# Two post-norm transformer layers on one core: the last gate/up step in halves, the high products of the first projection first, its weights in one piece, and new orders of the steps

## The reference, cut to what matters

```python
x = L0_attn_x                                   # (4, 256, 256)
x = _layernorm(x + _L0_attn_ref(x, w_project, w_out))              # 16 heads of 16, causal softmax
x = _layernorm(x + _L0_ffn_ref(x, gate_w, up_w, down_w, ...))      # silu(g) * u, 704 wide, ternary weights and scales
x = _layernorm(x + _L1_attn_ref(x, Wq, bq, Wk, bk, Wv, bv, Wo, bo))
x = _layernorm(x + _L1_ffn_ref(x, W_up, W_gate, W_down))           # 1024 wide, weights quantised to -1, 0, 1 times a scale
```

## Time and profile before

| | us |
|---|---|
| median of 3 runs | 256.35 (256.03 to 258.0) |
| profiled execution, its own time | 255.42 |
| its span, first to last instruction | 253.5 |
| PE busy | 240.6 |
| VectorE busy | 204.3 |
| GpSimd busy | 167.1 |
| ScalarE busy | 161.4 |

### The profile page before, as it was taken

One profiled execution on the slowest core, in us unless ns is written; L12 is line 12 of the kernel. 1 busy time (PEld: TensorE's weight loads), 2 busy tenths in 40 slices (PEclk: granted clock), 3 DMA queues, 4 the chain that ended last, 5 costly groups with the idle time before them and its releaser, 6 DMA issues.

```text
span 253.5 us, 6724 instructions
## 1 busy us (share of the span) xinstructions
PE 240.6 (95%) x2398; PEld 216.3 (85%) x2398; DVE 204.3 (81%) x599; ACT 161.4 (64%) x290; POOL 167.1 (66%) x218
## 2 busy tenths in 40 slices
PE   8998989999999999999999898998999999999991
PEld 8997967877789989989999897765788888999990
DVE  2477976999776876889999998998999975767664
ACT  4682465469889979627444567848788484555551
POOL 8763080528769854998637186599878885675663
PEclk9999999999999999999999999999999999999998
DMA  6867768542234343245626046055010000000003
GB/s 164 277 193 203 216 175 241 152 120 79 76 98 109 109 129 119 85 145 144 187 85 189 3 122 189 31 153 145 0 45 3 4 3 0 3 35 8 3 0 124
DMA packets 23312, 26.39 MB, mean 104 GB/s; under 512 B 3184, under 2 KB 18288, under 8 KB 23280
## 3 DMA queue, kind: packets, MB, share of 16 engines
q1 hardware_dynamic: 23136, 25.71, 35.2%
q10 hardware_dynamic: 144, 0.26, 0.3%
HBM read 12.20 MB, written 1.05 MB: 52 GB/s over the span
## 4 chain that ended last, share of the span: by engine, by line
PE 71%; POOL 6%; DVE 5%; DMA 5%; ACT 5%; issue 4%; SPq 2%; POOLq 0%; ACTq 0%
PE psum L566 9%; PE psum L567 8%; PE psum L568 8%; PE psum L686 6%; PE psum L661 5%; PE psum L741 5%; PE psum L742 5%; DMA k_stack<-k_part 3%; PE psum L629 3%; PE psum L689 2%; PE psum L633 2%; PE psum L664 2%; POOL hidden L1253 2%; PE psum L775 2%; PE psum L638 2%
## 5 line engine op out<-in xcount | busy, mean ns | idle before, releaser
L857 ACT ACTIVATE probs<-psum 128x768 f32<-128x768 f32 x64 | 49.1, 809 | 11.9 <-PE psum L667 5.9
L1253 POOL TENSOR_TENSOR hidden<-hf,hidden 128x512 fp32r<-128x512 f32 x24 | 31.6, 1320 | 13.5 <-ACT hidden L899 13.5
L1221 POOL TENSOR_SCALAR_AFFINE_SELECT probs<-probs 128x512 f32<-128x512 f32 x48 | 32.3, 688 | 10.1 <-ACT probs L857 9.7
L1009 DVE TENSOR_REDUCE block_max<-psum 128x6 f32<-128x768 f32 x32 | 28.9, 946 | 6.0 <-PE psum L633 5.9
L661 PE MATMUL psum<-q_stack,k_stack 98*128 98x256 bf16 x128 | 28.6, 274 | 2.1 <-DMA q_stack<-maxT_lo 1.0
L1020 DVE CUSTOM_DVE_ANT_0 masked<-psum,mask 128x256 bf16<-128x256 f32 x64 | 26.7, 418 | 1.6 <-issue 0.9
L1106 DVE SCALAR_TENSOR_TENSOR hf<-th,psum 128x512 f32<-128x512 f32 x28 | 18.9, 677 | 9.8 <-ACT th L888 3.9
L566 PE MATMUL psum<-xT_hi,gu_hi 128*128 128x256 f32 x88 | 25.3, 288 | 0.0
L567 PE MATMUL psum<-xT_lo,gu_hi 128*128 128x256 f32 x88 | 24.9, 283 | 0.0
L568 PE MATMUL psum<-xT_hi,gu_lo 128*128 128x256 f32 x88 | 24.9, 283 | 0.0
L664 PE MATMUL psum<-q_stack,k_stack 98*128 98x128 bf16 x128 | 24.7, 218 | 0.0
(11 more groups left out here) (167 smaller groups left out, 919.9 us busy)
## 6 DMA issues: line engine op xcount, KB each, us to landing
q_stack<-q_part SPq DMA_DIRECT2D x48, 128.0 KB, 2.7
k_stack<-k_part SPq DMA_DIRECT2D x48, 128.0 KB, 2.4
raw<-f SPq DMA_DIRECT2D x24, 256.0 KB, 3.0
raw<-a SPq DMA_DIRECT2D x8, 256.0 KB, 3.2
raw<-f0gu SPq DMA_DIRECT2D x4, 352.0 KB, 4.1
x<-x_nat SPq DMA_DIRECT2D x4, 256.0 KB, 5.4
raw<-f0dn SPq DMA_DIRECT2D x3, 256.0 KB, 3.0
out<-x SPq DMA_DIRECT2D x3, 256.0 KB, 2.3
```

The costliest lines, as they stand in the source:

```text
L857: nc.scalar.activation(probs[(n - 1) % 4][:, :, :], place(key)[:, :, 0:T + P], ACT.Exp, scale=SC).then_inc(exp_done, 1)
L1009: nc.vector.tensor_reduce(block_max[b % 2][:, 2 * i:2 * i + 2, 1:4], both(key)[:, :, 0:3 * P].rearrange("p j (c t) -> p j c t", t=P), mybi ...
L1221: pool.affine_select(out=diag, in_=diag, compare_op=ALU.is_ge, fill=0.0, base=0, pattern=[[0, 2], [0, 2], [1, P]], channel_multiplier=-1). ...
L1253: pool.tensor_tensor(hidden[(n - 1) % NHID][1][:, :, :], hf[n % 2][:, :].rearrange("p (a t) -> p a t", a=2), hidden[(n - 1) % NHID][0][:, ...
```

## The change

It has five parts.

1. QK:000 and QK:001 do their products in another order: four high by high products, which wait for the high parts alone, then four with xT_lo, then four with wa_lo. The number stays 12.
2. The four quarters of the weights a0, and those of a1, lie in memory so that a quarter is one row of 2 KB per partition; before, it was two rows of 1 KB.
3. The last gate/up step, GU:133, becomes GE:130 and GE:131, one tile of the hidden width each (8 matmuls, tanh of 256 columns, two products of 256 columns), HI:133 becomes HE:130 and HE:131, D:133 becomes DE:130 and DE:131 (4 matmuls each).
4. The last layer norm: VectorE does both halves' residuals, then both statistics, both aggregates and both additions of EPS, GpSimd the two powers; ScalarE normalises and stores the first half (NT:130), VectorE and SP the second.
5. All five lists of steps and BANKS are new.

```diff
 VECTOR_STEPS = """
-    XPARTS:000 PREPA:000-1 XPARTS:010 QK:000-1 XPARTS:020 XPARTS:030 QK:010 PREPA:002 QK:011 QK:020-1 PREPA:003
-    S:000-7 MB:000 S:010 MX:000 QK:030-1 S:011-6 SCALES:000 UT:000 IV:000 S:017 MB:010 S:020-1 MX:010 S:022 YM:000
+    PREPA:000-1 XPARTS:000 XPARTS:010 QK:000-1 XPARTS:020 QK:010-1 PREPA:002 QK:020-1 XPARTS:030 PREPA:003 S:000-7
+    MB:000 QK:030 S:010 MX:000 QK:031 S:011-5 SCALES:000 UT:000 IV:000 S:016-7 S:020 MB:010 S:021 UT:001 MX:010
...
 TENSOR_STEPS = """
-    QK:000 XI:010 QK:001 QK:010 XI:020 XI:030 QK:011 QK:020-1 V:000 V:010 S:000-4 QK:030 S:005-7 QK:031 S:010 MX:000
-    V:020 S:011-3 ST:000-1 S:014-5 ST:002-3 S:016 PV:000-1 ST:004-7 S:017 S:020-2 MX:010 PV:002-3 S:023-4 V:030
+    QK:000 XI:010 QK:001 XI:020 QK:010 XI:030 QK:011 QK:020-1 V:000 V:010 S:000-5 QK:030 S:006-7 QK:031 S:010 MX:000
+    S:011 V:020 S:012-4 ST:000 S:015 ST:001-3 S:016 PV:000-1 ST:004-7 S:017 S:020-1 PV:002-3 MX:010 S:022-5 V:030
...
-    GU:010-1 XT:020 XT:100 O:030 GU:012 QK:100 GU:020 D:010 XT:030 D:011-2 GU:021 QK:101 GU:022 XT:110 GU:030
-    QK:110-1 S:100-1 GU:031 S:102-3 D:020-1 S:104-5 D:022 GU:032 S:106-7 D:030-1 S:110 XT:120 V:100 S:111-2 MX:100
+    GU:012 GU:020 QK:100 XT:030 D:010-2 GU:021 QK:101 GU:022 XT:110 GU:030 QK:110-1 S:100-1 GU:031 S:102-3 D:020-2
+    S:104-5 GU:032 D:030 S:106-7 XT:120 D:031 S:110 V:100 MX:100 S:111 QK:120 S:112 D:032 S:113 QK:121 S:114 V:110
...
-    D:113 XT:230 GU:123 GU:130-1 D:120-2 GU:132-3 D:123 D:130-3
+    GU:130 D:120 GU:131 D:121-2 GU:132 D:123 GE:130-1 D:130-2 DE:130-1
...
 SCALAR_STEPS = """
...
-    GU:121 HI:120-1 XT:230 GU:122-3 GU:130 HI:122 GU:131 HI:123 HI:130-1 GU:132-3 HI:132-3 LN:310 LN:320
+    HI:121 XT:230 GU:122-3 GU:130 HI:122-3 GU:131 HI:130-1 GU:132 GE:130 HI:132 GE:131 HE:130-1 LN:310 LN:320 NT:130
...
 GPSIMD_STEPS = """
...
-    LN:020 LN:100 YT:030 HI:010 TERN:100 LN:030 TERN:101 HI:011 TERN:102 HI:012 SPLIT:100 TERN:103 LN:110 TERN:104-5
-    HI:020 SPLIT:101 HI:021-2 TERN:106 SPLIT:110 HI:030 SPLIT:111 HI:031 LN:120 HI:032 PREP1:003 TERN:107 LN:130
-    SPLIT:120-1 XC:100 ST:100-4 TERN:108 ST:105-7 XC:110 SPLIT:130-1 ST:110-5 YT:100 ST:116 TERN:109 ST:117 ST:120-1
+    HI:001-2 ST:035-7 LN:020 LN:100 YT:030 HI:010 TERN:100 LN:030 TERN:101 HI:011-2 TERN:102-3 SPLIT:100 LN:110
+    TERN:104 HI:020 TERN:105 SPLIT:101 HI:021 TERN:106 SPLIT:110 HI:022 HI:030 SPLIT:111 TERN:107 LN:120 HI:031-2
+    PREP1:003 LN:130 SPLIT:120-1 ST:100 XC:100 ST:101-2 XC:110 ST:103-7 SPLIT:130 TERN:108 ST:110 SPLIT:131 ST:111-5
...
 SYNC_STEPS = """
-    LOAD:001 LOAD:003 QK:000 LOAD:002 QK:001 MID:000-1 LO:000-1 QK:010 MID:010 LO:010 MID:011 QK:011 LO:011 LO:020
-    RAW:000-1 LOAD:000 MX:000 ML:000 LO:021 QK:020 MID:020-1 QK:021 RAW:002-3 MID:030 QK:030 MX:010 ML:010 MID:031
+    LOAD:001 QK:000-1 LOAD:003 LO:000-1 MID:000-1 MID:010 LO:010 QK:010-1 LO:011 MID:011 RAW:000-1 LO:020 LOAD:002
+    LOAD:000 MX:000 ML:000 LO:021 QK:020-1 MID:020-1 RAW:002-3 QK:030 MID:030-1 MX:010 ML:010 LO:030 QK:031 LO:031
...
-            c = slice(n * D, (n + 1) * D)
-            queue.dma_start(raw_a[:, :, c], a0[:, :, c]).then_inc(a0_in[n], 16)
+            queue.dma_start(raw_a[n], a0[:, n * KT * D:(n + 1) * KT * D]).then_inc(a0_in[n], 16)
...
                 if step == "QK":
+                    if (l, b) == (0, 0):
+
+                        o = take(key)
+                        for w, m, wait in ((wa_hi, xT_hi, ((wa0_hi, i + 1), (xT_hi_done, 1))), (wa_hi, xT_lo, ((xT_done, 1),)),
+                                           (wa_lo, xT_hi, ((wa0_lo, i + 1),))):
+                            for signal, value in wait:
+                                pe.wait_ge(signal, value)
+                            for j in range(2):
+                                for kt in range(KT):
+                                    last = nc.tensor.matmul(o[:, j * T:(j + 1) * T], w[:, kt, i * D + j * P:i * D + (j + 1) * P],
+                                                            m[:, kt, xcols(b)], start=w is wa_hi and m is xT_hi and (j, kt) == (0, 0),
+                                                            stop=w is wa_lo and kt == KT - 1, skip_group_check=True)
+                        last.then_inc(qk_mm, 1)
+                        continue
...
+                if step == "DE":
+
+                    pe.wait_ge(end_lo, i + 1)
+                    o, kt = parts_of(("D", l, b, 0)), MT1 - 2 + i
+                    h_hi, h_lo = hidden[LAST % NHID]
+                    for tt in range(TT):
...
+                if step == "NT":
+
+                    k_ = NLN % 2
+                    act.wait_ge(tail_offset, 1)
+                    nc.scalar.activation(x[:, TT * b, :], res[k_][:, 0, :], ACT.Identity, scale=rstd[k_][:, 0:1],
+                                         bias=offset[k_][:, 0:1]).then_inc(tail_scaled, 1)
+                    act.wait_ge(tail_scaled, 1)
+                    act.dma_start(out[:, TT * b:TT * b + 1, :], x[:, TT * b:TT * b + 1, :]).then_inc(stored, 16)
...
                 if step == "DT":
...
+                    for tt in range(TT):
+                        dve.wait_ge(tail_mm, tt + 1)
+                        nc.vector.scalar_tensor_tensor(res[k_][:, tt, :], parts_of(("D", l, b, 0))[:, tt, :], out_gain[:, 0:1],
+                                                       x[:, TT * b + tt, :], ALU.mult, ALU.add).then_inc(res_done, 1)
+                    for tt in range(TT):
+                        dve.wait_ge(res_done, 2 * NLN - 1 + tt)
+                        nc.vector.bn_stats(stats[k_][:, tt, :], res[k_][:, tt, :]).then_inc(stats_done, 1)
...
```

More of the change, by code:

```diff
@@ L60 @@
 MT1 = EXPERT // P
+LAST = NB * (-(-MT0 // 2) + MT1 // 2) - 1
 EPS = 1e-5
@@ L436, in xcols @@
             return slice(b * T, (b + 1) * T)
-        raw_a = raw[:, :].rearrange("p (k n) -> p k n", k=KT)
+        raw_a = [raw[:, n * KT * D:(n + 1) * KT * D] for n in range(4)]
         W0 = TILES0 * P // 2
@@ L714, in _ @@
                     last.then_inc(xt_mm, 1)
+                if step == "GE":
+                    o, mt = take(key), MT1 - 2 + i
+                    for part in range(2):
+                        for kt in range(KT):
+                            w = (gu_hi, gu_lo)[part][:, kt * EXPERT + mt * P:kt * EXPERT + (mt + 1) * P]
+                            oo = o[:, part * T:(part + 1) * T]
+                            nc.tensor.matmul(oo, w, xT_hi[:, kt, xcols(b)], start=(kt == 0), stop=False)
+                            last = nc.tensor.matmul(oo, w, xT_lo[:, kt, xcols(b)], start=False, stop=(kt == KT - 1))
+                    last.then_inc(end_mm, 1)
+                if step == "DE":
[3 more added lines that the diff above has]
+                    for tt in range(TT):
+                        tok = slice(tt * P, (tt + 1) * P)
+                        nc.tensor.matmul(o[:, tt, :], h_hi[:, i, tok], dn[:, kt * D:(kt + 1) * D], start=False, stop=False,
+                                         skip_group_check=True)
+                        last = nc.tensor.matmul(o[:, tt, :], h_lo[:, i, tok], dn[:, kt * D:(kt + 1) * D], start=False,
+                                                stop=(i == 1), skip_group_check=True)
+                        if i == 1:
+                            last.then_inc(tail_mm, 1)
                 if step == "GU":
@@ L875, in _ @@
                     last.then_inc(ln_done, 1)
+                if step == "GE":
+                    act.wait_ge(end_mm, i + 1)
+                    if i == 0:
+                        act.wait_ge(gated, LAST - 1)
+                    nc.scalar.activation(th[(LAST + 1) % 2][:, i * T:(i + 1) * T], place(key)[:, 0:T], ACT.Tanh,
+                                         scale=half[:, 0:1]).then_inc(end_tanh, 1)
+                if step == "HE":
+                    if i == 0:
+                        act.wait_ge(d_mm, LAST + 1 - NHID)
+                    act.wait_ge(end_hf, i + 1)
+                    nc.scalar.activation(hidden[LAST % NHID][0][:, i, :], hf[(LAST + 1) % 2][:, i * T:(i + 1) * T],
+                                         ACT.Copy).then_inc(end_hi, 1)
+                if step == "NT":
[5 more added lines that the diff above has]
+                    act.dma_start(out[:, TT * b:TT * b + 1, :], x[:, TT * b:TT * b + 1, :]).then_inc(stored, 16)
                 if step == "GU":
@@ L1083, in _ @@
                     residual("D", l, b, n, range(TT), out_gain[:, 0:1] if l else None)
+                if step == "GE":
+                    h_, o = hf[(LAST + 1) % 2][:, i * T:(i + 1) * T], place(key)
+                    dve.wait_ge(end_tanh, i + 1)
+                    if i == 0:
+                        dve.wait_ge(hl_done, LAST - 1)
+                    nc.vector.scalar_tensor_tensor(h_, th[(LAST + 1) % 2][:, i * T:(i + 1) * T], 1.0, o[:, 0:T],
+                                                   ALU.add, ALU.mult).then_inc(end_gated, 1)
+                    dve.wait_ge(end_gated, i + 1)
```

(9 more changed lines are left out.)

129 lines of the change are left out of this document (64 added, 65 removed), and 14 rows, old and new, of the table BANKS.

## The result

The changed kernel takes 259.22 us (median of 4 runs, 258.75 to 259.81) beside 256.19 (255.89 to 258.0) for the one before: ratio 1.0149, 95% interval 1.0109 to 1.0189. It is slower by 1.5%. The prediction was 255.5, no change, with a range up to 258.0 and 7% on slower: wrong, and outside its range. The profiled execution is the run of 258.75 us, span 257.0, which is 3.5 us more than the span of before. Executions of one kernel differ by about 1% either way, so a difference of some tenths between two single traces need not come from the edit.

The account below looks back on a forecast made before the run. PE was taken to set the pace, so only start, waits and tail could pay: +0.8 - 0.9 - 0.7 = -0.8 us, predicting 255.5 us against the median of 256.35, range 253.0 to 258.0.

Parts of the forecast that it names:

- What is A?: Start: landing time of the second weight piece, taken as 5.6 us, with ends 4.75 and 6.6.
- d: Start: how late QK:000's last product would come, 1.2 us, with ends 0.35 and 2.2.
- 19.9 + d: Start of S:000 by SP's chain of 13 DMA issues; PE's own chain gave 19.4 + d.
- The lower end of the start's range: Shift of S:000 by -0.5 us, from d = 0.35 on PE's chain; the upper end was +2.0.
- set these two against each other: ST:000: QK:030 before MX:000 lengthens the maxT_lo wait, one more S step (0.55 us) fills it; no net cost.
- high first: Start: QK:000's four high products first gain 0, since the warm-up keeps them from starting before 5.76 us.
- Both named waits: Middle: D:012's wait for the low half of hidden goes, -0.7 us; S:110's wait for k_stack shrinks, -0.2.
- Its reader on VectorE: Middle: TERN:102, 0.7 us later on POOL, delays nothing, as later readers on PE have a matrix step of slack.
- for all the other moved steps I take 0: Middle: remaining reordered steps cost or gain nothing, with bounds of -3.6 and +2 us.
- rival A: Start: second weight piece lands no earlier, QK:030 before MX:000 is not covered; +1.0 us in all, 257.4; chance 0.20.
- C: Rival: VectorE becomes the bound from 110 to 170 us; +2.1 us in all, 258.5; chance 0.12.
- B: Rival: the new orders close all those middle waits of PE; -3.5 us in all, 252.9; chance 0.15.

Follow-up runs that it names:

- e1: The changed kernel with the weight pieces again as two rows of 1 KB per partition; 259.22 us, ratio 1.0114.
- e5: The changed kernel with weight pieces as two rows of 1 KB and VectorE's XPARTS:000 again ahead of PREPA:000-1; 256.16 us, ratio 1.0009.
- e7: The kernel before with one swap in GpSimd's list, HI:012 ahead of TERN:102; 257.38 us, ratio 1.0078.
- e3: The kernel before with only the last gate/up step in halves and the new last layer norm; 255.43 us, ratio 0.9967.
- e8: The kernel before with the edits of e2, e6, e7 and e3 together; 258.71 us, ratio 1.0115.
- e11: The kernel before with e7's swap and, on VectorE, TERN:102 behind D:010 and XT:110 ahead of TERN:105; 258.45 us, ratio 1.0058.
- e12: The kernel before with the edits of e3 and the three moved entries of e11; 257.73 us, ratio 1.0038.
- e4: The changed kernel with VectorE's XPARTS:000 again ahead of PREPA:000-1; 256.76 us, ratio 1.0022.
- e2: The kernel before with each weight piece as one row of 2 KB, for a0 and a1; 258.48 us, ratio 1.0077.
- e6: The kernel before with one-row weight pieces and x_tr issued first of all, by SP instead of ScalarE's queue; 255.84 us, ratio 1.0009.
- e10: The kernel before with VectorE's PREPA:000-1 moved ahead of XPARTS:000; 260.62 us, ratio 1.0182.

## Why the prediction was wrong

**Start: forecast +0.8, measured +2.0 at S:000 and +2.4 at 35 us.** The failing step is "What is A?". I priced the landing of the second weight piece at 5.6 by the number of packets alone and held everything else in the sum fixed, the landing of x_tr among it. x_tr was the row of ScalarE just ahead of those I quoted, and it had no term. It landed 2.1 us later. ScalarE then had xT_hi and wa_hi[0] to do and reached wa_hi[1] at 6.60, done at 7.23. By the formula of the step, A + 0.63, this is A = 6.6, the late end: d was 2.2, and 19.9 + d gives 22.1 for S:000, measured 22.15. Of the 1.0 us by which A was missed, the piece's own landing (6.16) is 0.6 and the work held up by x_tr is 0.4. SP's 13 issues, too, were back to back from 10.56 on as reckoned, and one of them took 1.68 us again, for which I had taken some of the loss off. So the chain behind A was right. The lower end of the start's range was not: with the same formula d = 0.35 gives +0.1 on SP's chain and not the -0.5 of PE's. Another part of the loss, 0.4 us, comes behind S:000, where ST:000 waited 1.27 us for maxT_lo in place of 1.03 and QK:030 stood before MX:000 on VectorE; I had "set these two against each other". By the ratios the start weighs even more than by this one trace: undoing its two edits takes 1.0149 to 1.0009, about 3.6 us.

The sentence "the four high products cannot start before 5.76 either" does not hold: they started at 4.98 in e1 and at 5.27 in e5, where the same warm-up was done sooner. "The gain from 'high first' is 0" holds for the kernel as changed, since its high products started at 6.76. The two starts with wa_lo first suggest that the edit is worth something under that order, and in e5 QK:000 began at 5.27, ahead of the end of wa_lo[0] at 5.63, before a wait for x took the gain back; by itself it was not run.

The rule of the Trainium skill that I weighed (Perfetto Trace Analysis, DMA Optimizations: larger DMAs raise throughput) held for bytes in part: 324 GB/s in 4 to 5 us, before 199, but 87 against 155 in 1 to 3 us. It says nothing of which transfer comes first, and that was the cost.

**Middle: forecast -0.9, measured +1.3 to +1.4.** Both named waits went: at D:012 the lag falls by 0.9 (forecast 0.7), at S:110 by 0.8 (forecast 0.2). The failing steps are two. "Its reader on VectorE has D:010 and GU:020 behind it, whose readers on PE have a matrix step of slack" is false: e7 shows LN:110 and S:100 on that path, and a swap that loses 2 us in the kernel before. (In the changed kernel SPLIT:101 is on time, so there this path is not what cost.) And "for all the other moved steps I take 0": S:100 took back 1.3 (0.4 of it by one slow issue on SP; the rest is what was won at D:012, since its k_part comes no earlier), and 0.7 came at 54 us (a new wait of 0.65 for ScalarE's probs). A further 1.0 came at 77 us, for maxT_lo. That one is no proof against the new order, since e3, e8, e11 and e12 have it at 72 to 73 us (1.04 to 1.43) with the old one. From which of the many moved entries the 0.7 comes was not tried.

How much the middle costs is less sure than its sign. From 48 us to GU:132 the lag grows by 1.3 in the changed kernel, and by 1.8, 1.0 and 0.4 in e1, e4 and e5, which have the same lists there. In e2, e3, e6 and e10, with the lists of before, it changes by -0.4, +0.6, -0.3 and 0.0. And e5's ratio leaves middle and tail together between -0.7 and +1.2 us.

**Tail: forecast -0.7, measured -0.3.** Up to the residual the step was right: it starts 0.43 earlier (forecast 0.5), and D:132 has no wait. From the residual to the last write 3.39 us, before 3.65: 0.26 won, forecast 0.2. The failing step is "ScalarE writes and stores the other half from 249.8, earlier than SP's". It was only 0.14 us earlier (254.19 and 254.33), and from the end of the last write on VectorE to the end of the span there are 2.70 us, before 2.28. The two stores took 2.1 and 2.2 us to land, those of before 1.9.

**Rivals.** What came is rival A's start together with C's sign for the middle. A had the right place, VectorE's queue at 6.3 to 9 us, and the right size for it, +2.0, at a chance of 0.20. I took the -0.9 of the middle as given beside it, though. B did not come. C's total, 258.5, lies nearest to the 259.2 measured, but that is luck: its mechanism did not come, since VectorE is busy 57.35 of 60 us against 57.61, and most of the loss is at the start. The sign of error that I had named, new waits of over 1 us in 110 to 190, is in the trace.
